# ScalarE instead of VectorE makes the masked copies of the class rows in a graph-convolution kernel

## The chip, the core and the metric

The kernel runs on one core of a Trainium2 chip. A core has TensorE (PE, matrix products into PSUM), VectorE (DVE), ScalarE (ACT), GpSimd (POOL) and SyncE (SP, which issues the DMAs here). They run at the same time, each works through its own queue in order, and they wait for each other on semaphores. The metric is the device time of one execution in microseconds (us). Before the change it is 542.4 us, the median of three runs (542.37 to 543.49).

## What is computed

The input x has 32 batches of 256 rows with 1024 nodes each, and `adj` is a 256x256 matrix that both layers use as their weight.

```python
def _gc(x, adj, W, b):
    deg = adj.sum(axis=2, keepdims=True)
    h = x @ W.T + b
    return jnp.einsum('bij,bjh->bih', adj / deg, h)

h = jnp.maximum(_layernorm(x, axis=-1), 0.0)          # per row of 1024
g = _construct_adj(h, 8)            # graph over the 1024 nodes, from the mean over the 256 rows
y = jax.nn.relu(_gc(swapaxes(h, 1, 2), g, adj, b1))
y = _gc(y, g, adj, b2)
out = x + swapaxes(y, 1, 2)
```

The graph is built from an outer product of one vector with itself. So the nodes fall into a few classes whose neighbours are all the same, and the kernel never builds the 1024x1024 graph. For each layer it takes the product of the weight with the nodes' own values, and adds for each node a row that depends on its class alone ("class row").

## The kernel before

**Tiles and groups.** The 32 batches are handled in 8 groups of four. A batch has two halves of 512 nodes, so a group has eight units per layer and 16 in all. They are walked in four quarters: quarters 0 and 1 are layer 1, quarters 2 and 3 are layer 2. In each quarter the kernel also normalizes one batch of the next group. The order on every engine is written out by hand in its loop over g and q.

**PE.** `main` (L338) makes the twelve products of a unit: two output halves, two input halves, and three products of split float16 parts. `rows` (L350) adds the class rows of the unit with two more matmuls. The weights of these are the masked copies `l1w` (layer 1) or `l2w` (layer 2), one of 256 columns for each of the four batches, and the moving operand is `onehot`, the class of each node. The results lie in three PSUM buffers `ps`, so a unit can start only when the unit three before it has been read. In quarter 2 the first two units' `main`, then `times_q2` (L394, which makes the rows of layer 2), then the third unit's `main` are issued, and only then the `rows` of all three. In quarter 3 `plain_rows` (L377) makes layer 1's rows for the next group. At the start of the next group, behind its first unit, PE runs `times_q1` (L386).

**DVE.** `stats` (L755) and `mean_var` (L763) give the moments of a batch, `root_inverse` (L770) the reciprocal `r` of its standard deviation, `h_lo` (L777) the low part of the normalized values, `y_lo` (L783) the low part of a layer-1 unit, and `final` (L790) adds a layer-2 unit to x and frees its PSUM buffer. The top-eight search (L798 to L824), the classes (L829) and their degrees (L844, L848) are DVE's too.

**The class rows.** `r` counts 0 to 15: even for `l1w`, odd for `l2w`. They are 128 partitions by 256 columns. Each value is split into three bfloat16 parts that lie on different partitions. DVE reads the PSUM result and adds the bias (`rows_x`, L862), ScalarE rounds it to bfloat16 (`ra`, L501), DVE subtracts that where the partition wants a later part (`rows_t`, L866), ScalarE rounds again (`rb`, L503), and DVE subtracts once more (`lw`, L872). Then DVE makes four copies of `lw` (L876). Each is multiplied by a column of the constants `cs`, a number for each partition that is 1 on the 32 partitions of one batch and 0 elsewhere. PE's `rows` waits for the copy of its batch. On DVE, `mean_var`, a `final` and the reciprocal follow.

**ScalarE.** It makes the standard deviation (`root`, L455), the normalized values (L466) and their high part (L475), the relu of layer 1 (L487) and the roundings in `split_rows` (L501, L503). In both quarters where `split_rows` stands, `root` of the next batch comes right behind it.

**POOL.** `coefs` (L564 to L574) improves `r` by one Newton step, for which it waits for L770; `class_q1` (L612 to L623) makes the operand of PE's `times_q1` and stands behind `coefs` in its queue.

Of the kernel before, what the change touches and what calls it, by code (L numbers as in the profile page):

```python
# [5 lines left out]
ACT = mybir.ActivationFunctionType  # L6
# [23 lines left out]
GB = P // LANES  # L30
# [58 lines left out]
C_MINE = C_ISU + GB  # L89
# [3 lines left out]
def gnn_kernel(nc, x, adj_t, bias1, bias1_row, bias2_row, consts, out):  # L93
# [3 lines left out]
    with ExitStack() as ctx:  # L97
        def sb(name, shape, dt=F32):
            return ctx.enter_context(nc.sbuf_tensor(name, shape, dt))

        def sem(name):
            return ctx.enter_context(nc.semaphore(name))
# [8 lines left out]
        cs = sb("cs", [P, C_ALL])  # L111
# [56 lines left out]
        lw = sb("lw", [P, 2, S], BF16)  # L168
        l1w = sb("l1w", [P, GB, S], BF16)
        l2w = sb("l2w", [P, GB, S], BF16)  # L170
# [56 lines left out]
        row_w = sem("row_w")  # L227
        l1w_ready = sem("l1w_ready")
        l2w_ready = sem("l2w_ready")
# [211 lines left out]
        def _(act):  # L441
# [57 lines left out]
            def split_rows(r):  # L499
                act.wait_ge(row_x, r + 1)  # L500
                act.activation(ra[:], rx[:], ACT.Copy).then_inc(row_a, 1)  # L501
                act.wait_ge(row_t, r + 1)
                act.activation(rb[:], rt[:], ACT.Copy).then_inc(row_b, 1)  # L503

            def class_count(g):

                act.wait_ge(onehot_ready, g + 1)
                act.activation(kind[:], onehot[:, g % 2], ACT.Copy, accum_out=count[:]).then_inc(count_ready, 1)
# [6 lines left out]
            for g in range(-2, NG):  # L515
                for q in range(4):
# [14 lines left out]
                    if q == 2 and is_group(g):  # L531
                        split_rows(2 * g + 1)
                    if q == 3 and is_group(g + 1):
                        if g >= 0:
                            class_count(g + 1)
                        split_rows(2 * (g + 1))
# [212 lines left out]
        def _(dve):  # L749
# [118 lines left out]

            def rows_w(r):
                dve.wait_ge(row_b, r + 1)  # L870
                out_w, ready = (l1w, l1w_ready) if r % 2 == 0 else (l2w, l2w_ready)
                dve.scalar_tensor_tensor(lw[:, r % 2], rb[:], cs[:, C_NEG2:C_NEG2 + 1], rt[:],  # L872
                                         ALU.mult, ALU.add).then_inc(row_w, 1)
                dve.wait_ge(row_w, r + 1)
                for b in range(GB):
                    dve.tensor_scalar(out_w[:, b], lw[:, r % 2], cs[:, C_MINE + b:C_MINE + b + 1], None, ALU.mult  # L876
                                      ).then_inc(ready, 1)

            def make_scale():

# [51 lines left out]
            for g in range(-2, NG):  # L932
# [54 lines left out]
                if here:  # L987
                    rows_w(2 * g + 1)
# [39 lines left out]
                if to:  # L1028
                    rows_w(2 * (g + 1))
# [37 lines left out]
```

## Time and profile before

| | |
|---|---|
| median of 3 runs | 542.4 us (542.37 to 543.49) |
| the profiled execution, its time | 543.15 us |
| its span (first to last instruction) | 541.2 us |
| PE busy | 443.0 us, 82% |
| DVE busy | 428.2 us, 79% |
| ACT busy | 271.5 us, 50% |
| POOL busy | 195.6 us, 36% |
| mean granted clock of TensorE | 0.988 |

The busy time of an engine is the sum of its instructions' spans. The chain of waits follows the last instruction back, at each step to what released it; PE has 52% of it and DVE 31%. In the rows below every time is in us from the start of the span, unless it is said to be in ns. "[0.95 <-DVE xs L790]" means that the engine sat idle for 0.95 us and that the end of L790's write of `xs` ended it. PEld is the weight load of PE, PEclk the granted clock as a share of 2.4 GHz.

### The profile page before, as it was taken

Reading aid. Unit: us, or ns where it says so; the run is one execution under the profiler, and the core shown is the slowest. Engines: PE = TensorE matmul, PEld = TensorE weight load, DVE = VectorE, ACT = ScalarE, POOL = GpSimd, SP = SyncE. Lnnn points to the kernel's source line nnn. Section 1 sums busy time; section 2 is a strip of 40 time slices with the busy share of each in tenths; the row PEclk is TensorE's granted clock in tenths of the full one; section 3 lists DMA queues with packets and bytes.
Section 4 is the critical chain, followed back from the end, with each engine's and each line's share of the span. In section 5 each row is a group of like instructions: output and inputs, shape, how many; then the busy total and the mean of one; then the engine's idle time right before and its main releaser. Section 6 shows DMA issues by size and latency. Waiting matters only on the chain.

```text
span 541.2 us, 7336 instructions
## 1 busy us (share of the span) xinstructions
PE 443.0 (82%) x2188; PEld 200.8 (37%) x2188; DVE 428.2 (79%) x780; ACT 271.5 (50%) x564; POOL 195.6 (36%) x873
## 2 busy tenths in 40 slices
PE   1002058999899979999899989998999799999995
PEld 0000024444344434443444444443444344444442
DVE  3857965899979997999799988999599956763362
ACT  2655446754576437743774567544673364014300
POOL 1021536162444425262617062634426251414100
PEclk9999997999999999999999999998999999999999
DMA  8970000005810584037600880078104410141034
GB/s 281 411 285 0 1 1 1 1 2 191 291 63 1 189 264 171 0 94 283 247 1 23 289 311 1 2 254 295 73 1 140 172 78 1 78 173 61 1 142 169
DMA packets 18807, 68.20 MB, mean 126 GB/s; under 512 B 1744, under 2 KB 2384, under 8 KB 18768
## 3 DMA queue, kind: packets, MB, share of 16 engines
q1 hardware_dynamic: 18768, 67.73, 34.1%
q8 instruction: 18, 0.29, 0.2%
q14 instruction: 21, 0.17, 0.1%
HBM read 34.17 MB, written 33.55 MB: 125 GB/s over the span
## 4 chain that ended last, share of the span: by engine, by line
PE 52%; DVE 31%; POOL 7%; ACT 4%; issue 3%; DMA 1%; SPq 0%; POOLq 0%
PE ps L338 41%; DVE xs L790 9%; PE ps L350 6%; DVE hl L777 5%; DVE bn L755 5%; PE pf L363 3%; PE pm L386 2%; POOL nw L564 2%; ACT hf L466 2%; DVE kind L822 1%; DVE fv L817 1%; PE pm L394 1%; ACT hl L475 1%; DVE rt L866 1%; DVE lw L872 1%
## 5 line engine op out<-in xcount | busy, mean ns | idle before, releaser
L338 PE MATMUL ps<-hl,wh 128*128 128x512 f16 x1024 | 308.7, 384 | 9.9 <-DVE xs L790 9.9
L338 PE MATMUL ps<-hl,wl 128*128 128x512 f16 x512 | 196.1, 383 | 0.0
L338 PEld LDWEIGHTS ps<-hl,wh 128*128 128x128 f16 x1024 | 98.4, 99 | 134.4 <-DVE xs L790 16.7
L783 DVE SCALAR_TENSOR_TENSOR hl<-ps,hl 128x1024 f16<-128x1024 f32 x64 | 78.2, 1222 | 50.1 <-ACT hl L487 49.6
L466 ACT ACTIVATE hf<-xs,nbias,rstd 128x1024 f32<-128x1024 f32 x64 | 79.1, 1236 | 74.6 <-POOL nbias L574 74.3
L487 ACT ACTIVATE hl<-ps 128x512 f16<-128x512 f32 x128 | 74.8, 589 | 77.5 <-PE ps L350 77.5
L777 DVE TENSOR_TENSOR hl<-hf,hl 128x1024 f16<-128x1024 f32 x64 | 77.5, 1210 | 19.3 <-ACT hl L475 19.2
L790 DVE SCALAR_TENSOR_TENSOR xs<-ps,sc,xs 128x1024 f32<-128x1024 f32 x64 | 80.0, 1261 | 9.4 <-PE ps L350 9.1
L755 DVE BATCH_NORM_STATS2 bn<-xs 128x6 f32<-128x512 f32 x128 | 82.0, 680 | 4.3 <-DMA xs<-x_dram 4.3
L338 PEld LDWEIGHTS ps<-hl,wl 128*128 128x128 f16 x512 | 50.5, 99 | 61.8 <-issue 2.4
L475 ACT ACTIVATE hl<-hf 128x1024 f16<-128x1024 f32 x64 | 67.6, 1057 | 2.0
L564 POOL TENSOR_TENSOR nw<-r 128x2 f32<-128x2 f32 x32 | 13.3, 417 | 126.6 <-DVE r L770 126.6
L588 POOL COPY gat<-hl 128x4 f16 x256 | 47.2, 236 | 24.6 <-DVE idx L813 15.3
L363 PE MATMUL pf<-hl,ones_h 128*32 128x512 f16 x256 | 18.5, 412 | 32.2 <-DVE hl L777 31.4
L694 POOL COPY hl<-yhl 128x32 f16<-128x32 f16 x32 | 6.9, 228 | 100.5 <-DVE hl L783 100.0
L350 PE MATMUL ps<-onehot,l1w 128*128 128x512 bf16 x128 | 38.1, 379 | 0.0
L350 PE MATMUL ps<-onehot,l2w 128*128 128x512 bf16 x128 | 35.6, 380 | 1.7 <-DVE l2w L876 1.7
L377 PE MATMUL pm<-wt,q1r 128*128 128x256 f32 x32 | 9.3, 416 | 21.8 <-POOL q1r L599 21.8
L487 ACT ACTIVATION_READ_ACCUMULATOR hl<-ps 128x1 f32 x128 | 25.3, 198 | 0.0
L455 ACT ACTIVATE std<-mv,eps 128x2 f32<-128x2 f32 x32 | 9.4, 293 | 30.1 <-DVE mv L763 30.1
L363 PEld LDWEIGHTS pf<-hl,ones_h 128*32 128x32 f16 x256 | 5.7, 100 | 43.8 <-DVE hl L777 32.1
L386 PE MATMUL pm<-q,wt 128*128 128x64 f32 x64 | 9.6, 298 | 13.0 <-POOL q L623 13.0
(118 smaller groups left out, 391.7 us busy)
## 6 DMA issues: line engine op xcount, KB each, us to landing
xs<-x_dram SPq DMA_DIRECT2D x64, 512.0 KB, 7.0
out_dram<-xs SPq DMA_DIRECT2D x32, 1024.0 KB, 5.0
wt<-adj_t_dram SPq DMA_DIRECT2D x1, 256.0 KB, 4.4
b1r<-b_row_dram SPq DMA_DIRECT2D x1, 128.0 KB, 5.5
b2r<-b_row_dram SPq DMA_DIRECT2D x1, 128.0 KB, 5.9
cs<-consts_dram SPq DMA_DIRECT2D x1, 86.5 KB, 4.1
b<-b_dram SPq DMA_DIRECT2D x1, 1.0 KB, 3.9
```

The source lines that it names most:

```text
L338: pe.matmul(ps[i % 3][:, m], w[:, k, o], hl[:, slot, part, k, cols], start=(k == 0 and w is wh and part == 0), stop=False)
L350: last = pe.matmul(ps[i % 3][:, m], w[:, m * P:(m + 1) * P], onehot[:, g % 2, cols], start=False, stop=True)
L363: last = pe.matmul(pf[o, :], ones_h[:, 0:LANES], hl[:, n % NHL, part, k, cols], start=(k == 0 and part == 0), stop=(k == KC - 1 and part = ...
L466: act.activation(hf[:, c % NHF], xs[:, n % NX, k], ACT.Relu, bias=nbias[:, n % RB, k:k + 1], scale=rstd[:, n % RB, k:k + 1], accum_out=s_a ...
L475: act.activation(hl[:, n % NHL, 0, k], hf[:, c % NHF], ACT.Copy).then_inc(hi_ready, 1)
L487: last = act.activation(hl[:, n % NHL, 0, m, half * HALF:(half + 1) * HALF], ps[i % 3][:, m], ACT.Relu, accum_out=acc[:, g % 2, half, m, L ...
L564: pool.tensor_tensor(nw[:, 0], r, r, ALU.mult).then_inc(newton, 1)
L588: pool.tensor_copy(gat[:, j, t], hl[:, slot, :, :, bass.ds(v, 1)].rearrange("p a k o -> p a (k o)")).then_inc(gathered, 1)
L755: dve.bn_stats(bn[:, n % 2, k, half], xs[:, n % NX, k, half * HALF:(half + 1) * HALF]).then_inc(stats_done, 1)
L777: dve.tensor_tensor(hl[:, n % NHL, 1, k], hf[:, c % NHF], hl[:, n % NHL, 0, k], ALU.subtract).then_inc(lo_ready, 1)
L783: dve.scalar_tensor_tensor(hl[:, n % NHL, 1, :, cols], ps[place(1, n, half) % 3][:], 0.0, hl[:, n % NHL, 0, :, cols], ALU.max, ALU.subtrac ...
L790: dve.scalar_tensor_tensor(xs[:, n % NX, :, cols], ps[place(2, n, half) % 3][:], scal(S_C2), xs[:, n % NX, :, cols], ALU.mult, ALU.add).th ...
```

## The change

ScalarE's `split_rows` gets the four masked copies. It waits for DVE's `lw` (semaphore `row_w`) behind its second rounding, and makes them with the activation `Copy` and the same column of `cs` as scale. DVE keeps `lw` and loses the copies and the wait in front of them. The semaphores that PE waits for, and their counts, are the same.

```diff
@@ split_rows (ScalarE)
                 act.activation(ra[:], rx[:], ACT.Copy).then_inc(row_a, 1)
                 act.wait_ge(row_t, r + 1)
                 act.activation(rb[:], rt[:], ACT.Copy).then_inc(row_b, 1)
+                out_w, ready = (l1w, l1w_ready) if r % 2 == 0 else (l2w, l2w_ready)
+                act.wait_ge(row_w, r + 1)
+                for b in range(GB):
+                    act.activation(out_w[:, b], lw[:, r % 2], ACT.Copy, scale=cs[:, C_MINE + b:C_MINE + b + 1]
+                                   ).then_inc(ready, 1)
@@ rows_w (VectorE)
                 dve.wait_ge(row_b, r + 1)
-                out_w, ready = (l1w, l1w_ready) if r % 2 == 0 else (l2w, l2w_ready)
                 dve.scalar_tensor_tensor(lw[:, r % 2], rb[:], cs[:, C_NEG2:C_NEG2 + 1], rt[:],
                                          ALU.mult, ALU.add).then_inc(row_w, 1)
-                dve.wait_ge(row_w, r + 1)
-                for b in range(GB):
-                    dve.tensor_scalar(out_w[:, b], lw[:, r % 2], cs[:, C_MINE + b:C_MINE + b + 1], None, ALU.mult
-                                      ).then_inc(ready, 1)
```

## Rows read from the trace of the kernel before

**Rows 1.** The page's busy times: us, share of the span, instructions.

```profile
PE 443.0 (82%) x2188; PEld 200.8 (37%) x2188; DVE 428.2 (79%) x780; ACT 271.5 (50%) x564; POOL 195.6 (36%) x873
```

**Rows 2.** The chain of waits, 230 to 260: start, us, engine, tile, line.

```profile
233.81 0.87 DVE l2w L876 x4
...
234.88 1.20 DVE xs L790
...
253.87 1.09 POOL nw L564
...
258.46 1.10 PE pm L386 x8
```

**Rows 3.** Groups by line: busy us, mean ns of one, idle before.

```profile
L876 DVE TENSOR_SCALAR l1w<-lw,cs 128x256 bf16<-128x256 bf16 x32 | 7.0, 283 | 0.3
L503 ACT ACTIVATE rb<-rt 128x256 bf16<-128x256 f32 x16 | 6.7, 416 | 13.9 <-DVE rt L866 13.9
```

**Rows 4.** Timeline of ScalarE near the start: start, us, engine, line.

```profile
9.54 0.63 ACT L445 ACTIVATE hf<-wt 128x512 f32<-128x512 f32 x1 [7.32 <-DMA b2r<-b_row_dram]
...
21.98 1.06 ACT L475 ACTIVATE hl<-hf 128x1024 f16<-128x1024 f32 x1
22.95 1.23 ACT L466 ACTIVATE hf<-xs,nbias,rstd 128x1024 f32<-128x1024 f32 x1
...
26.44 0.71 ACT L449 ACTIVATE wh<-wt,sc 128x512 f16<-128x512 f32 x1
```

**Rows 5.** Timeline, odd rows of one group (quarter 2).

```profile
233.30 0.47 DVE L872 SCALAR_TENSOR_TENSOR lw<-rb,cs,rt 128x256 bf16<-128x256 bf16 x1
...
234.15 1.47 PE L350 MATMUL ps<-onehot,l2w 128*128 128x512 bf16 x6 [0.22 <-DVE l2w L876]
...
234.79 1.28 DVE L790 SCALAR_TENSOR_TENSOR xs<-ps,sc,xs 128x1024 f32<-128x1024 f32 x1
234.91 0.29 ACT L455 ACTIVATE std<-mv,eps 128x2 f32<-128x2 f32 x1 [1.68 <-DVE mv L763]
...
237.13 0.16 DVE L770 RECIPROCAL r<-std 128x2 f32<-128x2 f32 x1
```

**Rows 6.** Timeline, even rows of the same group (quarter 3).

```profile
250.99 0.47 DVE L872 SCALAR_TENSOR_TENSOR lw<-rb,cs,rt 128x256 bf16<-128x256 bf16 x1
...
252.48 1.23 DVE L790 SCALAR_TENSOR_TENSOR xs<-ps,sc,xs 128x1024 f32<-128x1024 f32 x1
252.60 0.29 ACT L455 ACTIVATE std<-mv,eps 128x2 f32<-128x2 f32 x1 [2.27 <-DVE mv L763]
253.63 0.15 DVE L770 RECIPROCAL r<-std 128x2 f32<-128x2 f32 x1
...
253.77 0.60 PE L338 MATMUL ps<-hl,wh 128*128 128x512 f16 x2 [0.95 <-DVE xs L790]
```

**Rows 7.** Timeline, the first even rows.

```profile
76.99 0.88 DVE L876 TENSOR_SCALAR l1w<-lw,cs 128x256 bf16<-128x256 bf16 x4
...
78.10 0.29 ACT L455 ACTIVATE std<-mv,eps 128x2 f32<-128x2 f32 x1 [2.28 <-DVE mv L763]
...
78.43 0.17 DVE L770 RECIPROCAL r<-std 128x2 f32<-128x2 f32 x1 [0.36 <-ACT std L455]
...
83.26 1.97 PE L386 MATMUL pm<-q,wt 128*128 128x64 f32 x8 [4.03 <-POOL q L623]
```

**Rows 8.** Timeline, the last group's odd rows.

```profile
518.16 1.47 PE L350 MATMUL ps<-onehot,l2w 128*128 128x512 bf16 x6 [0.19 <-DVE l2w L876]
```

**Rows 9.** Waits in total, longest; the chain's longest pieces; 8-us windows (busy, PEclk).

```profile
PE pm L386 <- POOL q L623: 13.0, 7, 4.0
...
259.56 2.59 PE ps L338 x12
...
374.74 4.28 PE ps L338 x12
...
253.00:261.00 8.00, 5.74 (x30) 3.01 (x31) 7.94 (x11) 4.44 (x10) 4.18 (x16) 1.00 0.80 265
...
368.00:376.00 8.00, 5.56 (x27) 2.79 (x28) 7.94 (x11) 4.34 (x11) 4.08 (x15) 0.93 0.78 256
```

## Prediction

> **What bounds the kernel now.** I read the chain of waits first, then the timeline around the two places where the class rows are made, then ScalarE's rows. The busy shares alone (PE 82%, DVE 79% [rows 1]) don't say which engine counts. The chain says that they take turns, with a period of about 57.6 us for each group of four batches. From the matmul L386 (258.46) PE runs almost without a gap until the layer-2 rows. There it waits for DVE's masked copy l2w (233.81). From PE's first layer-2 rows on, DVE is the chain: the `final` at 234.88 and everything behind it in DVE's queue, up to the reciprocal `r` of L770. POOL then computes coefficients and q1 (253.87 on), and PE's L386 has been waiting for that [rows 2]. So an edit counts in two places: where it moves the *first* copy of l2w, and where it moves `r` of L770 in the fourth quarter of a group.
>
> **Part 1: the price of a copy on ScalarE.** On DVE one copy takes 0.283 us and four take 0.87. On ScalarE a 128x256 copy without a scale from memory takes 0.416 [rows 3]. The new copies read their scale from `cs`, one number for each partition. The only pair that shows this price is L445 against L449: both 128x512, the first with no scale from memory 0.63, the second with one 0.71, so about 0.08 more. That makes 0.49 us for a copy. Consecutive ScalarE instructions overlap: L475 starts at 21.98 and takes 1.06, L466 starts at 22.95, 0.09 before its end [rows 4]. So I take c = 0.49 for one copy and s = 0.40 from start to start. The bounds are s = 0.33 (0.416 less 0.09, no price for the scale) and s = 0.49 (no overlap between copies that are 0.49 long). I take the middle one since both of its pieces have a row.
>
> The Trainium skill, "ScalarE: Activation LUTs", section "What ACT_TABLE_LOAD costs", gives a fixed part, a price per element and 93 ns for each operand read through a pointer, and says that consecutive ones overlap by 93 ns; that would be an estimate of 0.49 and 0.40. Its section "Rules for kernel authors" gives multiplications to VectorE. By the row L503 alone the sum below would be about 1.5 us below zero, by the page about 1 above; the row L449 sides with the page, though it is a single instruction.
>
> **Part 2: odd rows (l2w), 8 times.** DVE's lw starts at 233.30, ends at 233.77; the first copy starts 0.04 later and PE starts at 234.15 after 0.22 of waiting [rows 5]. ScalarE is idle here behind rb and can start at the same 233.81; it also stands in its queue at this place. Its first copy ends 0.49 - 0.28 = 0.21 us later, and so do PE's rows and the `final` at 234.79, which starts when two of these matmuls are done. The DVE time given back here (four copies) is worth nothing: DVE would wait for that `final` anyway. Everything behind on DVE moves by 0.21. The second copy (needed 1 us later by PE) is hidden. ScalarE's square root of L455 waits in its queue behind four copies: 234.91 becomes 233.81 + 4 x 0.40 = 235.4, but `r` is only made at 237.13, so 1.4 us of cover remain. In the two last groups the same copy stands before PE [rows 8], so all eight count: 8 x 0.21 = **+1.7 us**.
>
> **Part 3: even rows (l1w) with DVE crowded, 6 times.** DVE's lw starts at 250.99 and ends at 251.46. Then come four copies, the mean and variance, the `final` at 252.48 and `r` at 253.63 [rows 6]. Without the copies (0.87, less some 0.07 of overlap with what follows) all but `r` moves up by 0.8. PE had waited 0.95 for that `final`, and 0.15 of this wait is left. But this is not what the group ends on: PE then waits for POOL's q anyway, and POOL for `r`. `r` needs the square root L455, which now stands behind the copies: it starts at 251.50 + 4 x 0.40 = 253.10 instead of 252.60, takes 0.29, and `r` follows at about 253.44. So `r` comes 0.19 earlier, not 0.8, and DVE idles for the difference, with h_lo, class degrees and two `final`s queued behind `r`. The wait that was removed (DVE's copies) is replaced by one for ScalarE. 6 x -0.19 = **-1.1 us**. As a formula, `r` moves by 4s - 1.79; between s = 0.33 and 0.49 this is -0.47 to +0.17 each time. l1w itself is needed only behind the next unit's products (from 253.77 on, twelve matmuls, 2.6 us), so its lateness is hidden.
>
> **Part 4: the first even rows, once.** At the start DVE isn't crowded. `r` at 78.43 follows the square root at 78.10 directly, and this follows the copies of 76.99 [rows 7]. On ScalarE the copies end the wait at 77.00 + 1.60 = 78.60: **+0.5 us** (4s - 1.10), straight into PE's wait of 4.03. The eighth even row (about 478) has no square root behind it and nobody waiting: 0.
>
> Sum of the queues: 1.7 - 1.1 + 0.5 = **+1.1 us**. With c = s + 0.09 it is 36s - 13.4: zero at s = 0.37, -1.5 at 0.33. With copies of 0.49 that don't overlap it is +3.6.
>
> **Part 5: PE's clock.** In part 3 PE finishes its unit some 0.6 us sooner against `r`, so its wait before L386, 1.5 us in the steady groups (13.0 in 7 waits, 4.03 the longest), becomes 1.5 + 0.8 - 0.2 = 2.1. This wait has a price in the trace. After the wait of 4.03 the granted clock was low. In one of the six steady groups (368 to 376, granted 0.93, against 1.00 in the others) PE fell to its lower level, 1.2 GHz, behind this same wait: twelve matmuls took 4.28 instead of 2.59, 1.7 us lost [rows 9]. One in six at 1.5 us, one in one at 4.0: on a straight line 2.1 us gives 0.37, or 2.2 of six groups, 1.2 more than now. I take one more: **+1.7 us**. Its bounds are -1.7 (the present one goes, as the phase falls) and +5 (three more).
>
> **The forecast.** +1.1 + 1.7 = +2.7 us. Against the profiled execution (span 541.2, time 543.15, with one such low stretch in it) that is 545.9. The median of the runs is 542.4, 0.75 below the profiled one, so I forecast 542.4 + 2.7 = **545.1 us**.
>
> **Rivals.**
> *The queues alone.* No further low stretch: 542.4 + 1.1 = 543.4. For it: five of six groups stayed at full clock behind 1.5 us, and 2.1 is nearer to that than to 4.
> *Faster: the scale costs nothing on ScalarE.* Place: the square root behind l1w. Price: s = 0.33, so `r` comes 0.47 earlier six times (-2.8), the start loses 0.2 and l2w 8 x 0.13, sum -1.5: 541.0 with the clock unchanged (it has a longer wait then too). It decides from s below 0.37. For it: L503 is the same size and type of output. Against: L449.
> *The copies don't overlap,* since each signals a semaphore: +3.6, 546.0. Against: L475 and L466 signal too and overlap.
> *Two or more further low stretches:* 546.8 or more. For it: the line above is drawn through two points only.
> *The change doesn't act,* since DVE waits elsewhere for as long in both places: 542.4.
>
> **Chances.** One more low stretch 0.33; queues alone 0.32; scale for nothing 0.13; two or more 0.10; no overlap 0.07; no effect 0.05. The measurement tells about 0.2%, 1.1 us, from no change. The queues alone lie right at this bound, so I give a third of them to slower. Slower: 0.33 + 0.10 + 0.07 + 0.10 = 0.60; faster 0.13; the rest, 0.27, within. The range 541.6 to 546.9 leaves out some of the faster rival's lower half and of the two or more low stretches. The forecast's own range is 544.3 to 545.9.
>
> **What would show it.** ScalarE's copies: 0.49 each, four in 1.7. PE's wait for l2w up by 0.21 in each of eight groups. DVE's `r` waiting for std in the fourth quarter, six more times, by some 0.5. POOL's coefficients 0.2 earlier after lw than before. PE's wait for the `final` down from 0.95 to about 0.1 and its wait before L386 up to 2.1. DVE's busy time down by 14 (7.0 for l1w, as much for l2w), ScalarE's up by about 26 (64 x 0.40). The granted clock low in one steady group more. It would be wrong if `r` came nearly 0.8 earlier, which needs a square root that is not held by the copies, or if the clock stayed up.

## The result, and the profile after

| | before | changed |
|---|---|---|
| median of 17 runs each | 543.53 us (542.37 to 545.73) | 547.31 us (543.63 to 552.87) |
| ratio, 95% interval | | 1.0064 (1.004 to 1.0088) |
| the profiled execution, its time | 543.15 us | 543.89 us |
| its span | 541.2 us | 542.0 us |
| DVE busy | 428.2 us | 415.2 us |
| ACT busy | 271.5 us | 297.7 us |

The change made the kernel slower by 3.5 us (2.2 to 4.8, from the ratio). The ratio leaves out the changed kernel's two slowest runs (552.4 and 552.9, counted as slow ones); the medians of all runs, which the rest of the text uses, are 3.8 us apart. The sign was forecast, and so was the size of the change (+2.7), but the time of 547.3 lies above the range of 541.6 to 546.9. Two things of the table matter. With 14 more runs the kernel before has a median of 543.5, not the 542.4 of its first three. And the changed kernel's runs spread over 9 us, so the profiled execution, at the fast end, shows only 0.7 us of the cost (543.89 against 543.15).

What that execution shows is the queues. First the timeline of the odd rows (start, us, engine, line, operation), which answers to [rows 5]:

```profile
233.56 0.47 DVE L876 SCALAR_TENSOR_TENSOR lw<-rb,cs,rt 128x256 bf16<-128x256 bf16 x1
...
234.07 1.70 ACT L507 ACTIVATE l2w<-lw,cs 128x256 bf16<-128x256 bf16 x4 [0.57 <-DVE lw L876]
...
234.63 1.47 PE L350 MATMUL ps<-onehot,l2w 128*128 128x512 bf16 x6 [0.44 <-ACT l2w L507]
...
235.28 1.28 DVE L795 SCALAR_TENSOR_TENSOR xs<-ps,sc,xs 128x1024 f32<-128x1024 f32 x1 [1.04 <-PE ps L350]
```

The instructions of L507 (duration in ns: least, median, most) answer to [rows 3]:

```profile
L507 ACT ACTIVATE l2w<-lw,cs x32: 491/493/508, 118.9 to 519.5; 128x256 bf16<-128x256 bf16 x32
```

One copy takes 0.493 us, four take 1.70. PE's wait for the first copy went from 0.22 to 0.44, and DVE now idles 1.04 before the `final`: the time it was given back here is worth nothing. From the start of lw to this `final` it is 1.72 us, before it was 1.49, so 0.23 later.

The timeline of the even rows in the same group, which answers to [rows 6]:

```profile
251.47 0.47 DVE L876 SCALAR_TENSOR_TENSOR lw<-rb,cs,rt 128x256 bf16<-128x256 bf16 x1
...
251.97 1.71 ACT L507 ACTIVATE l1w<-lw,cs 128x256 bf16<-128x256 bf16 x4 [1.17 <-DVE lw L876]
...
252.06 1.23 DVE L795 SCALAR_TENSOR_TENSOR xs<-ps,sc,xs 128x1024 f32<-128x1024 f32 x1
...
253.59 0.28 ACT L455 ACTIVATE std<-mv,eps 128x2 f32<-128x2 f32 x1
253.90 0.17 DVE L775 RECIPROCAL r<-std 128x2 f32<-128x2 f32 x1 [0.61 <-ACT std L455]
...
258.73 1.79 PE L386 MATMUL pm<-q,wt 128*128 128x64 f32 x8 [2.19 <-POOL q L628]
```

The `final` follows lw's start by 0.59 instead of 1.49. But the square root (`std`) stands behind the copies, DVE waits 0.61 for it, and `r` follows lw's start by 2.43 instead of 2.64: 0.21 gained, not 0.9. PE's wait before L386 grew to 2.19.

The first even rows, answering to [rows 7]; here lw starts at 76.46, before at 76.49:

```profile
78.57 0.28 ACT L455 ACTIVATE std<-mv,eps 128x2 f32<-128x2 f32 x1
78.88 0.17 DVE L775 RECIPROCAL r<-std 128x2 f32<-128x2 f32 x1 [1.75 <-ACT std L455]
```

The waits in total (us, times, longest), which answer to the first of [rows 9]:

```profile
PE pm L386 <- POOL q L628: 17.6, 7, 4.5
...
DVE r L775 <- ACT std L455: 10.1, 9, 3.4
...
PE ps L338 <- DVE xs L795: 4.1, 8, 0.5
...
PE ps L350 <- ACT l2w L507: 3.5, 8, 0.4
```

The same waits in the kernel before:

```profile
PE ps L338 <- DVE xs L790: 9.9, 14, 1.0
...
DVE r L770 <- ACT std L455: 5.1, 3, 3.5
...
PE ps L350 <- DVE l2w L876: 1.7, 8, 0.2
```

PE's wait for `final` shrank from 9.9 us in 14 waits to 4.1 in 8, and most of what it saved stands in the wait before L386 (17.6 now, 13.0 before). `r` waits for the square root in nine places, three before.

The clock is in the 8-us window around that L386 (length, then busy time and count of PE, PEld, DVE, ACT and POOL, then PEclk, DMA share and GB/s) and in the chain behind it:

```profile
253.00:261.00 8.00, 5.76 (x26) 3.18 (x25) 7.32 (x11) 4.85 (x13) 3.85 (x14) 0.87 0.86 300
```

```profile
258.73 1.79 PE pm L386 x8
260.52 3.57 PE ps L338 x12
```

The granted clock fell to the lower level (1.2 GHz) right behind the wait: the eight small matmuls took 1.79 instead of 1.10 and the next twelve 3.57 instead of 2.59, 1.7 us in all. Apart from group 0, where the clock is low behind L386 in both traces, it falls nowhere else in this one. It is one steady group of six, as in the profiled execution before: the one low group more that was forecast isn't in this trace. The other runs have no trace, only a mean clock. In the 17 runs it goes from 0.988 (543.6 us) to 0.975 (552.9 us), with a mean of 0.983; a straight line through them gives 0.57 us for each 0.001 of clock and leaves about 1 us of scatter. So the clock isn't the whole of the spread: the median run, 547.31, has 0.987, hardly less than the run of 543.89.

The profiled executions of all kernels, those of the experiments too, give a scale for this mean. With no low steady group it is 0.992 to 0.997, with one 0.988 to 0.990, with three 0.981, with five 0.975. By this estimate, 0.983 stands for two to three low groups in the changed kernel, and the mean of the kernel before, 0.989, for one.

### The profile page after: what moved, and what is told of

The parts are those of the page before. It is cut to its first block, busy times and chain, and to the rows that moved or that the text cites. A ratio compares the mean times of both kernels' runs of the same rounds, so it can differ in the third digit from the quotient of the medians.

```text
span 542.0 us, 7336 instructions
## 1 busy us (share of the span) xinstructions
PE 442.8 (82%) x2188; PEld 201.3 (37%) x2188; DVE 415.2 (77%) x716; ACT 297.7 (55%) x628; POOL 194.9 (36%) x873
## 4 chain that ended last, share of the span: by engine, by line
PE 53%; DVE 27%; POOL 7%; ACT 6%; issue 3%; DMA 1%; SPq 0%; POOLq 0%
PE ps L338 40%; DVE xs L795 7%; PE ps L350 6%; DVE hl L782 5%; DVE bn L760 5%; PE pf L363 3%; ACT l1w L507 2%; PE pm L386 2%; POOL nw L569 2%; ACT hf L466 2%; DVE kind L827 1%; DVE fv L822 1%; PE pm L394 1%; ACT hl L475 1%; DVE rt L871 1%
## 5 line engine op out<-in xcount | busy, mean ns | idle before, releaser
L386 PE MATMUL pm<-q,wt 128*128 128x64 f32 x64 | 10.3, 313 | 17.6 <-POOL q L628 17.6
L350 PEld LDWEIGHTS ps<-onehot,l2w 128*128 128x128 bf16 x128 | 11.9, 98 | 20.6 <-ACT l2w L507 7.4
```

Source lines behind the costliest of these rows:

```text
L350: last = pe.matmul(ps[i % 3][:, m], w[:, m * P:(m + 1) * P], onehot[:, g % 2, cols], start=False, stop=True)
```

## The experiments

Theory 1: the queues cost about +1.1 us, as forecast, and the rest is TensorE's clock, which falls behind the longer wait before L386. The rival: the excess over the queues comes from ScalarE or from contention, in runs that the one profile doesn't show. The kernel before was measured again beside each set: medians of 543.81 (first four kernels), 543.95 (the next four), 543.51 (the two after) and 543.26 (the last). The ratios below are against these.

**Filling the wait.** In front of L386, PE gets matmuls whose result nobody reads, fewer than fit in its wait.

```diff
+            def filler(g, count):
+                if g >= 1 and is_group(g + 1):
+                    pe.wait_ge(fv_copied, NH * (g + 1))
+                    for _ in range(count):
+                        pe.matmul(pf[:], ones_h[:], wh[:].rearrange("p k s -> p (k s)"), start=True, stop=True)
...
                     if i == 0:
+                        filler(g, 8)          # 6 in the kernel before
                         times_q1(g)
```

> The changed kernel with eight more matmuls (128x512, into the PSUM bank of the means, which is free there; their result is overwritten and never read) in front of L386 in groups 1 to 6, 1.7 us of work inside a wait of 2.2. Theory 1 (what the change costs beyond its queues is TensorE's clock, which falls behind this longer wait): no low stretch in the steady groups, mean granted clock 0.990 or more in every run, lowest and highest run within 1.5 us, and the time is that of the kernel before with fillers plus 1.1 us, about 542.7. Rival (the excess comes from ScalarE's queue or from contention in runs that the one profile doesn't show): 546 to 547 still, with a spread of several us.

> The kernel before with six such filler matmuls (1.3 us inside a wait of 1.5). Theory 1: the low stretches that the kernel before has in about one group of six go too: 541.5 us, 2 us under the median of the kernel before (543.5), spread under 1.5 us. Rival: 543.5 as without fillers, or more, since PE's queue has more to do.

Measured: the changed kernel with fillers 543.22 us (541.24 to 544.61, ratio 0.9986, 0.9964 to 1.0008), the kernel before with fillers 541.92 (540.49 to 542.69, ratio 0.9965, 0.9943 to 0.9986). The difference is 1.3 us, the queues' part. Matmuls that do nothing took 4.1 us off the changed kernel, and all its twelve runs have a clock of 0.990 or more, 0.992 in the mean instead of 0.983; at 0.57 us for 0.001 that is 5.6 us, an estimate, so the clock is enough to explain the 4.1. Neither profiled execution with fillers has a low stretch in groups 1 to 6. The spread is 3.4 us, not the 1.5 expected: in the profiled execution the transfer of x in one group took 7.07 us and stood in the chain, which the fillers don't touch. That group took 58.36 us instead of 57.61, so this is a part of the spread at most.

**One half at a time.** In `split_rows` and `rows_w` the copies are made by the one engine or the other, by the row's parity:

```diff
+                if r % 2 == 1:                # 0 in the second kernel; VectorE has the other rows
                     act.wait_ge(row_w, r + 1)
                     for b in range(GB):
                         act.activation(out_w[:, b], ...
```

> Only the copies of l2w (odd rows) on ScalarE, those of l1w back on VectorE. Theory 1: the first copy is 0.22 us later before PE in eight groups, +1.8 us; the wait before L386 stays 1.5 us, so the clock and the spread are those of the kernel before: ratio 1.003, 545.3. Rival (the clock plays no part, the cost sits in ScalarE's queue for both kinds alike): half of the whole excess, +1.9, but with the wide spread of the changed kernel.

> Only the copies of l1w (even rows) on ScalarE, those of l2w on VectorE as before. Theory 1: queues -0.2 x 6 + 0.5 = -0.7 us, but the wait before L386 is 2.2 us as in the changed kernel, so the wide spread and the clock's cost of about 2.5 us stay: +1.8, ratio 1.003, mean clock down to 0.980 in some runs. Rival (the clock plays no part): 0.7 us faster than before, 542.8, spread as before.

Measured: odd rows alone 543.62 (542.27 to 547.06, ratio 0.9998, 0.9973 to 1.0023); even rows alone 547.85 (547.21 to 550.78, ratio 1.009, 1.0055 to 1.0125). The half that saves queue time costs the most. This goes against the rival, but it misses both of theory 1's numbers too: odd rows came out 1.7 us under the 545.3 expected, even rows 2.6 over it. The chain's pieces at L386, first of the even rows alone, then of the odd rows alone:

```profile
145.50 1.48 PE pm L386 x8
146.97 3.89 PE ps L338 x12
...
261.93 1.82 PE pm L386 x8
263.75 3.53 PE ps L338 x12
...
320.98 1.10 PE pm L386 x8
...
378.36 1.10 PE pm L386 x8
...
435.73 1.57 PE pm L386 x8
437.30 3.80 PE ps L338 x12
```

```profile
202.39 1.10 PE pm L386 x8
...
260.19 1.10 PE pm L386 x8
```

A group without a low stretch takes 57.38 with even rows alone (378.36 - 320.98), 57.80 with odd rows alone, and 57.59 before. So each half does to the queues what was forecast, -0.2 and +0.2. Three of six groups are low in the first kernel, one of six in the second.

**The halves with the wait filled.** Six fillers with odd rows alone, eight with even rows alone.

> Copies of l2w alone on ScalarE, with six filler matmuls before L386. Odd rows alone had shown no cost (ratio 0.9998) where 1.8 us were expected. Theory 1: the queue cost is there, and a lower clock cost in those runs hid it; without the clock it shows: 541.9 (the kernel before with fillers) + 1.8 = 543.7. Rival (l2w's lateness is absorbed): 541.9.

> Copies of l1w alone on ScalarE, with eight filler matmuls before L386. Even rows alone were 1.009 of the kernel before. Theory 1 (all of that and more is the clock behind the longer wait): 541.9 - 0.7 = 541.2, ratio 0.995. Rival (ScalarE's later square root costs something by itself): over 544.

Measured: 544.02 (542.62 to 545.24, ratio 0.9996) and 541.03 (539.99 to 542.43, ratio 0.9946, 0.9924 to 0.9969). Against 541.92 that is +2.1 and -0.9, and their sum, +1.2, is the whole change's 1.3. The mean clocks of the filled kernels are not quite equal (0.991 to 0.994), so each of these differences is good to about 1 us only, an estimate by the slope above; the firmer sign of the queue costs are the periods of 57.38 and 57.80 us. The queue cost of the odd rows is there; their kernel without fillers happens to pay nothing for the clock. Even rows alone pay 6.8 us for it (547.85 against 541.03), more than the 4.1 of the whole change, though both have the same wait of 2.19 us before L386.

**The length of the wait at one period.** The changed kernel with three fillers instead of eight.

> The changed kernel with three filler matmuls before L386 instead of eight: 0.65 us of work, so that PE's idle time there is about 1.5 us, as in the kernel before, at the changed kernel's own period of 57.6 us. The period is that of the kernel before too, so this leaves the length of the wait as the only difference. Theory 1 (at one period, the clock's cost goes by how long PE idles there): the cost falls from 4.1 us to the 1.9 of the kernel before, 543.2 + 1.9 = 545.1. Rival (any wait gives the same, only a full one removes it): 547.

Measured: 544.98 (543.26 to 546.75, ratio 1.0028, 1.0006 to 1.0049), as expected. With 2.2 us idle the clock costs 4.1 us (547.3 - 543.2), with 1.54 it costs 1.8.

**The square root first.** If the queued square root is what ate the gain, its order is the remedy. On ScalarE:

```diff
                     if n is not None:
                         root(n + 1)
+                    if q == 3 and is_group(g + 1):
+                        masked_rows(2 * (g + 1))      # waits for lw, four copies into l1w
```

> Only the copies of l1w (even rows) on ScalarE, and there behind the square root of the next batch (L455) instead of in front of it; the copies of l2w stay on VectorE. Theory 1 (what held back the gain was the square root queued behind four copies): DVE's r of L770 comes 0.8 us earlier in six groups and at the start, the wait before L386 stays 1.5 us, so the clock costs what it costs before: 7 x -0.8 = -5.6 us, ratio 0.990. Rival (DVE's chain is bound elsewhere by then, say by ScalarE's normalized values or the fourth quarter's transfers): -1.2 us or less, as with the square root behind the copies.

On VectorE, without any change of engine:

```diff
+            def masked_rows(r):               # the wait for lw and the copies, taken out of rows_w
...
                     rows_w(2 * g + 1)
+                    masked_rows(2 * g + 1)
...
                     inverse_degrees(g + 1)
+                    masked_rows(2 * (g + 1))
```

> All copies on VectorE as before, but those of l1w moved from in front of the mean and variance to behind the class degrees, so nothing changes engines. Theory 1: the same as with the square root first, r comes 0.8 us earlier seven times, -5.6 us, since only what stands in front of r counts and the copies are hidden behind it: ratio 0.990. Rival (the gain needs VectorE to be rid of the work, as 79% busy suggests): under 2 us, since the copies now delay two final operations that PE's next units wait for.

Measured: 540.25 (535.98 to 542.63, ratio 0.9927, 0.9899 to 0.9954) and 541.88 (538.22 to 546.65, ratio 0.9955, 0.993 to 0.9981). Both are faster, and both gain less than the 5.6 us expected, with a wide spread. The timeline of the first:

```profile
247.43 0.47 DVE L879 SCALAR_TENSOR_TENSOR lw<-rb,cs,rt 128x256 bf16<-128x256 bf16 x1
...
248.13 0.29 ACT L455 ACTIVATE std<-mv,eps 128x2 f32<-128x2 f32 x1 [1.37 <-DVE mv L771]
248.33 1.69 ACT L508 ACTIVATE l1w<-lw,cs 128x256 bf16<-128x256 bf16 x4
...
249.16 0.16 DVE L778 RECIPROCAL r<-std 128x2 f32<-128x2 f32 x1
...
253.99 1.10 PE L386 MATMUL pm<-q,wt 128*128 128x64 f32 x8 [1.49 <-POOL q L631]
```

Now `r` follows lw's start by 1.73 instead of 2.64, a gain of 0.91, and PE's wait before L386 is 1.49 as before. What is missing from the expected time should then be the clock again, at a wait that had cost 1.8 us elsewhere; the next two kernels test this for it.

The VectorE version took 2.1 us off (543.95 to 541.88), close to its rival's "under 2 us", and it was not run with fillers. Its trace speaks for theory 1 all the same. That trace is of its slowest run (546.65 us, clock 0.975), with the clock low in five steady groups of six, and the one group without a low stretch reads:

```profile
261.02 1.10 PE pm L386 x8
...
317.81 1.10 PE pm L386 x8
```

That is 56.79 us, against 57.59 before: 0.8 us gained in a group with every copy still on VectorE. So what counts here is the order in front of `r`, and not the engine. In its eleven runs the time goes with the mean clock (538.2 at 0.991, 546.7 at 0.975), as it would if the clock took back the rest, but no fillers tested it.

**The same with the wait filled,** six fillers, first in groups 1 to 6, then in group 0 too (`if g >= 0`).

> The l1w copies on ScalarE behind the square root, with six filler matmuls before L386 in groups 1 to 6. Undisturbed groups of that kernel took 56.7 us against 57.6, but its runs spread from 536.0 to 542.6. Theory 1 (queues gain 0.9 in six groups and 1 at the start, the clock takes much of it back): 541.9 - 6.4 = 535.5, ratio 0.985, spread under 3 us, clock 0.990 or more. Rival (the spread has another source than PE's wait before L386): 540 with the same spread.

> The same with six fillers in group 0 too, where the wait before L386 is 2.2 us and PE has just begun its steady work. Theory 1 (waits before L386 alone pull the clock down): the low stretch behind the first L386 (twelve matmuls in 4.2 instead of 2.6) goes as well, 1.5 us less: 534.0. Rival (the clock is low there since PE had little to do for 20 us before, and six fillers at the lower level are longer than the wait): no gain, 535.5 to 536.

Measured: 534.70 (532.91 to 536.57, ratio 0.9838, 0.9808 to 0.9869) and **532.98** (532.66 to 534.52, ratio 0.9803, 0.9774 to 0.9833), 10.5 us under the kernel before measured beside it (543.51) and 14.3 under the changed kernel. The mean clock of the latter's six runs is 0.997 to 0.998. Its timeline at one L386 (L402 are the fillers), and two pieces of its chain:

```profile
250.36 0.59 PE L350 MATMUL ps<-onehot,l1w 128*128 128x512 bf16 x2
250.79 1.46 PE L402 MATMUL pf<-wh,ones_h 128*128 128x512 f16 x6
252.47 1.10 PE L386 MATMUL pm<-q,wt 128*128 128x64 f32 x8 [0.22 <-POOL q L638]
```

```profile
252.47 1.10 PE pm L386 x8
...
309.17 1.10 PE pm L386 x8
```

The fillers leave 0.22 us of the wait and delay nothing. A group takes 56.70. The step from the first to the second of these kernels, 1.7 us, is the size expected, but the intervals overlap, and the profiled execution of the first had a full clock at group 0 as well, behind a wait of 3.29 us. So that part is likely, not shown.

## Why the prediction failed, step by step

**The price of a copy** (part 1): right. A copy took 0.493 us against 0.49, four of them 1.70 against 1.7; the row L449 was the better guide than L503.

**Odd rows** (part 2): right, 0.22 us in each of eight groups against 0.21 forecast; by itself, with the wait filled, it measured +2.1 us against +1.7.

**Even rows and the start** (parts 3 and 4): right. `r` came 0.21 us earlier against 0.19, 2.42 us after lw's start in the first even rows instead of 1.94, which is +0.48 against +0.5, and half of the change alone gave -0.9 against -0.6. That the queued square root is what ate the gain was tested by moving it: `r` came 0.9 earlier and the group took 56.7 us.

**The sum of the queues:** +1.3 us with the wait filled, +1.1 forecast. That they agree to 0.2 is partly luck, as each filled kernel is known to about 1 us; the two profiled executions, with one low group each, differ by 0.8 in their spans. DVE's busy time fell by 13.0 us, not 14, a miss on which no term of the sum rests. The rivals that the scale costs nothing, that the copies don't overlap, and that nothing happens fall with it.

**The clock** (part 5) is the term that was mis-sized. The mechanism was the one named, low stretches behind the longer wait before L386, but it was given +1.7 us. By kernels that differ in fillers alone it costs the changed kernel 4.1 us (547.3 against 543.2) and the kernel before 1.6 to 1.9 (543.5 to 543.8 against 541.9), so the change pays +2.2 to +2.5. The fault lies in how the size was found: "one in six at 1.5 us, one in one at 4.0: on a straight line". One execution showed one low group of six, and I took this for a rate, and the second point of the line came from the first group, whose wait is of another kind (PE had been busy for only 7.2 of the 20 us up to 80). The line gave 1.2 groups more and I took one; the runs' mean clock speaks for one to two more. The length of the wait alone doesn't set the price either. The same 1.5 us of waiting cost nothing measurable with odd rows alone (543.6 against 544.0 with fillers), 1.6 to 1.9 us in the kernel before, and 5.5 us with the square root first (540.2 against 534.7). The same 2.2 us cost 4.1 in the changed kernel and 6.8 with even rows alone.

**The base** failed beside it: the forecast was set on the median of three runs, 542.4. The miss of 2.2 us is 1.1 of base, 0.2 of queues, and the rest, about 0.9, clock. The measured time lies 0.4 above the range, so the base alone would have brought it inside. So would the bound of part 5 (+5, three more low groups), which gives 542.4 + 1.1 + 5 = 548.5 and was left out of the range.

**What stays open:** why kernels with the same wait pay so differently. They differ in their period, from L386 to L386: 57.8, 57.6 and 56.7 us at the wait of 1.5 (costs of 0, 1.8 and 5.5), 57.6 and 57.4 at the wait of 2.2 (4.1 and 6.8). The low stretches fall on different groups, and no run changed the period alone. Also open is what makes up to 3 us between runs of nearly the same mean clock. That the length of the wait counts at one period is shown by the pair with eight and three fillers.

## What to carry to other kernels

Moving work off a crowded engine helps only as far as what is queued behind it on the *new* engine isn't on the chain: put the short operation that others wait for first, and the copies behind it, and the same four copies gain 0.9 us in a group instead of 0.2. Time saved ahead of a wait of PE makes that wait longer, and it can come back as a lower clock; matmuls that do nothing, a little shorter than the wait, are a cheap way to measure that share, and here also to win it back. A base of three runs, and a count from one profiled execution, are not a median and not a rate: take the spread of the runs, with their clocks, before putting a bound on such a term.

## What the runs showed of the hardware

Behind an idle stretch of 1.5 to 2.2 us in front of L386, and during or after the eight small matmuls of L386 (1.1 us), the granted clock was at its lower level in one to five of the six steady groups of each profiled execution without fillers. In the changed kernel PE had been busy for 53.3 of the 56 us before (202 to 258). Whether the small matmuls have a part in it, no run shows. Each such stretch cost 1.7 us. With the idle stretch cut to 0.5 us or less, no profiled execution had one. At group 0 the clock was once at full level behind 3.29 us of idling, and low behind 2.21 in another kernel. A ScalarE operation that reads its scale from memory took 0.077 us longer than one of the same size with none (0.493 against 0.416, and 0.706 against 0.629; the types of the operands differ in both pairs).
